# Instance-norm statistics from the loaded rows: VectorE sums and four transposes in place of sixteen matmuls

## The reference

```python
def _masked_instance_norm(x, mask):
    x = x * m                                   # m: [1, 512], over positions
    n_valid = jnp.sum(m, axis=-1)
    mean = jnp.sum(x, axis=-1) / n_valid        # one per channel
    var = jnp.sum(x * x, axis=-1) / n_valid - mean * mean
    return (x - mean) / jnp.sqrt(relu(var) + 1e-5) * m

q, k, v = Wq x + bq, Wk ctx + bk, Wv ctx + bv
attn = softmax(q k / 4, masked)
mean = attn v
std  = sqrt(relu(attn (v * v) - mean * mean))
out  = (_masked_instance_norm(x) * std + mean) * mask
```

## Time and profile before

| | us |
|---|---|
| median of 3 runs | 4275.7 (4275.27 to 4277.73) |
| the profiled execution, its own time | 4275.91 |
| its span in the trace | 4274.3 |
| first layer, from the span's start to the first instruction of the second | 703.7 |
| one batch in the steady part, g2 n = 1 to the same place of the next batch | 80.56 |

### The profile page before, as it was taken

The page is one execution under the profiler, slowest core; times in us unless marked ns, Lnnn a source line. Parts: engine busy times, 40 slices in busy tenths (PEclk is TensorE's granted clock), DMA queues, the critical chain, the costliest instruction groups (busy, mean ns, idle before and its releaser), DMA issues. The chain is left out here.

```text
span 4274.3 us, 68335 instructions
## 1 busy us (share of the span) xinstructions
PE 3998.9 (94%) x20812; PEld 3013.6 (71%) x20812; DVE 2939.8 (69%) x6467; ACT 1935.0 (45%) x3782; POOL 1592.7 (37%) x1094
## 2 busy tenths in 40 slices
PE   6999996789999987999999999999999999999999
PEld 2333333557777755887987887977988877878866
DVE  5667663688888893775757766757757757757643
ACT  3555553223333322555552555543555534545522
POOL 1334332456666651232235332344332244332330
PEclk8999998999999998999999999999999999999999
DMA  5434433000000002222223222223221123121222
GB/s 152 128 111 118 130 89 129 5 11 16 16 16 16 11 11 73 70 60 79 62 65 104 71 65 76 65 62 107 65 85 60 55 74 96 60 90 61 58 79 96
DMA packets 159993, 298.65 MB, mean 70 GB/s; under 512 B 19780, under 2 KB 42820, under 8 KB 158544
## 3 DMA queue, kind: packets, MB, share of 16 engines
q1 hardware_dynamic: 158000, 290.86, 22.1%
q0 software_dynamic: 1008, 3.67, 0.2%
q10 hardware_dynamic: 752, 1.23, 0.1%
HBM read 254.28 MB, written 42.21 MB: 69 GB/s over the span
## 5 line engine op out<-in xcount | busy, mean ns | idle before, releaser
L2176 POOL TENSOR_TENSOR c_wl<-c_wr,c_wh 128x512 fp32r<-128x512 f32 (+1 forms) x576 | 822.5, 1440 | 1640.8 <-ACT c_wh L2543 1384.6
L2644 ACT ACTIVATE c_pr<-c_ps,c_nms 128x257 f32<-128x257 f32 x512 | 244.5, 477 | 484.3 <-DVE c_nms L2866 482.4
L1700 DVE TENSOR_TENSOR_SCAN b_sb<-b_wt,b_s,b_ps 128x256 f32<-128x256 f32 x512 | 361.6, 736 | 16.0 <-PE b_ps L1153 4.1
L652 ACT ACTIVATE a_ex<-a_ps 128x1024 f32<-128x1024 f32 x256 | 260.9, 1022 | 212.8 <-PE a_ps L481 212.8
L763 DVE TENSOR_REDUCE a_nm<-a_ps 128x2 f32<-128x1024 f32 x256 | 311.5, 1221 | 60.7 <-PE a_ps L461 59.1
L1651 POOL TENSOR_TENSOR b_sb<-b_sb,b_rt 128x1024 f32<-128x1024 f32 x128 | 278.3, 2181 | 155.7 <-DVE b_sb L1700 113.3
L2543 ACT ACTIVATE c_wh<-c_wr 128x512 fp32r<-128x512 f32 (+1 forms) x464 | 315.4, 687 | 44.5 <-PE c_ps L2263 40.7
L2261 PE MATMUL c_ps<-c_hh,c_wh 128*128 128x512 f32 x768 | 309.3, 403 | 12.4 <-DVE c_hl L2750 11.9
L2261 PE MATMUL c_ps<-c_gh,c_wh 128*128 128x512 f32 x768 | 308.1, 401 | 5.4 <-DVE c_gl L2908 2.7
L2263 PE MATMUL c_ps<-c_hh,c_wl 128*128 128x512 f32 x768 | 304.3, 396 | 0.0
L2262 PE MATMUL c_ps<-c_hl,c_wh 128*128 128x512 f32 x768 | 304.0, 396 | 0.0
(11 more groups left out here) (371 smaller groups left out, 10078.7 us busy)
## 6 DMA issues: line engine op xcount, KB each, us to landing
c_wr<-in_downs SPq DMA_DIRECT2D x192, 256.0 KB, 2.7
c_wr<-in_wv SPq DMA_DIRECT2D x64, 512.0 KB, 4.0
c_wr<-in_wk SPq DMA_DIRECT2D x128, 256.0 KB, 2.9
c_wr<-in_wq SPq DMA_DIRECT2D x128, 256.0 KB, 2.7
a_qp<-strips SPq DMA_DIRECT2D x64, 256.0 KB, 4.1
a_kp<-strips SPq DMA_DIRECT2D x64, 256.0 KB, 4.9
c_wr<-in_fc SPq DMA_DIRECT2D x64, 256.0 KB, 2.8
strips<-a_qh SPq DMA_DIRECT2D x32, 256.0 KB
```

The costliest lines, as they stand in the source:

```text
L652: act.activation(EX[:, n % 4, :, :], ps[:, BT + 2 * (n % 2):BT + 2 * (n % 2) + 2, :], ACT.Exp).then_inc(ex_ready, 1)
L1700: mm = dve.tensor_tensor_scan(SB[:, quad % RING, pr % 2, e, 1:L + 1], WT[:, third(b, i), e, :], half(spread_bank(pair), e), S0[:, b % 2, 2 ...
L2176: pool.tensor_tensor(piece(WL, slot), piece(WR, slot), piece(WH, slot), ALU.subtract).then_inc(piece_cut[slot], 1)
L2644: act.activation(PR[:, i, 0:L + 1], ps[:, BS + 1 - i % 2, 0:L + 1], ACT.Exp, bias=NMS[:, i:i + 1], scale=float(K2) ** -0.5, accum_out=RS[: ...
```

## The change

The sums over positions are now made by DVE along the rows of `X`, which has channels on partitions. Each of four `tensor_tensor_reduce` writes a 128x512 product and adds it up into one column: x times the mask (`sum_inputs`, g1 n = 0 and 4, L751) and its square (`sum_squares`, g1 n = 3 and 5, L755). `column_moments` (g3 n = 4) makes mean and variance out of the columns, ACT takes the root of 128x2 numbers, DVE its reciprocal (`inverse_root`, now g0 n = 6). PE turns the columns into rows with four transposes, at the place of the sixteen matmuls, and DVE copies the bank once (`take_rows`). POOL's `normalize` subtracts and multiplies in one place in g3; `centre`, `scale`, `mask_x`, `moments`, `spread_of_x` and the squares on ACT are gone. Besides, the roots move from g0 n = 5 to n = 3, ahead of `qh`; the keys' projections from n = 4 to n = 5; `cut_x` and `cut_c` are cut in halves at two steps; `square_values` goes from n = 2 to n = 6, and that of g0 ahead of `take_pair`; SP loads the transposed x later; and the last batch's output is made by POOL for groups 0 to 2 and by DVE for group 3. Line numbers from L745 on in the diff's new functions are those of the new kernel.

```diff
-        TURN_AT, OLD_PAIR_AT, QUERIES_AT, KEYS_AT, PAIR_AT = 1, 2, 3, 4, 6
+        TURN_AT, OLD_PAIR_AT, QUERIES_AT, KEYS_AT, PAIR_AT = 1, 2, 3, 5, 6
...
                 place_maxima(b, 3)
-                load_statistics(b + 1)
                 load_inputs(b + 2)
...
                 place_maxima(b + 1, 0)
+                load_statistics(b + 1)
                 place_strips(b + 1, 3)
...
-            def centre(b):
-                pool.wait_ge(var_x, b + 1 + AHEAD)
+            def normalize(b):
+                pool.wait_ge(st_read, b + 1 + AHEAD)
                 pool.sem_inc(passed, 1)
-                pool.tensor_tensor(XM[:, :, :], XM[:, :, :], ST[:, 0:1, :].broadcast_to([P, EC, L]), ALU.subtract)
-                pool.drain().then_inc(centred, 1)
-
-            def scale(b):
-                pool.wait_ge(rstd_ready, b + 1 + AHEAD)
+                pool.wait_ge(stats_x_in, (b + 1) * N_STATS + AHEAD)
                 pool.sem_inc(passed, 1)
-                pool.tensor_tensor(XM[:, :, :], XM[:, :, :], ST[:, 3:4, :].broadcast_to([P, EC, L]), ALU.mult)
+                pool.tensor_tensor(XM[:, :, :], XT[:, :, :], ST[:, 0:1, :].broadcast_to([P, EC, L]), ALU.subtract)
+                pool.drain().then_inc(stats_read, 1)
+                pool.tensor_tensor(XM[:, :, :], XM[:, :, :], ST[:, 1:2, :].broadcast_to([P, EC, L]), ALU.mult)
                 pool.drain()
...
                     spread_out(prior)
-                    scale(prior)
...
                 group_moments(b, 2)
-                centre(b)
+                normalize(b)
                 if further:
                     cut_x(b + 2)
...
             group_3(B - 1, False, False)
+            cols = slice(0, (G0 - 1) * CG)
+            pool.wait_ge(std_ready, B + AHEAD)
+            pool.sem_inc(passed, 1)
+            pool.tensor_tensor(XM[:, :, cols], XM[:, :, cols], VAR[:, :, cols], ALU.mult)
+            pool.drain()
+            pool.tensor_tensor(XM[:, :, cols], XM[:, :, cols], MEAN[:, :, cols], ALU.add)
+            pool.drain()
+            for c in range(EC):
+                pool.tensor_scalar(OUT[:, c, cols], XM[:, c, cols], MCOL[:, c:c + 1], None, ALU.mult)
+            pool.drain().then_inc(parts_out, 1)
...
             def statistics(b):
-                pe.wait_ge(stats_in, b + 1 + AHEAD)
-                pe.wait_ge(sq_ready, b + 1 + AHEAD)
+                pe.wait_ge(cols_ready, b + 1 + AHEAD)
...
-                for c in range(EC):
-                    pe.matmul(ps[:, BX, 0:L], ONES[:, :], XM[:, c, :], start=(c == 0), stop=(c == EC - 1), skip_group_check=True)
-                for c in range(EC):
-                    mm = pe.matmul(ps[:, BX, L:2 * L], ONES[:, :], XQ[:, c, :], start=(c == 0), stop=(c == EC - 1), skip_group_check=True)
+                for i, k in itertools.product(range(2), range(LC)):
+                    mm = pe.transpose(ps[:, BX, i * L + k * P:i * L + (k + 1) * P], COLS[:, i, k:k + 1].broadcast_to([P, P]), ID[:, :])
                 mm.then_inc(st_ps, 1)
...
+                    if g == 0 and n == 0 and not first:
+                        square_values(b, 0)
                     if n == 0 and not first:
...
-                    if g == 0 and more and n == 0:
-                        cut_c(b + 1)
-                    if n == 2 and g + 1 < G0:
+                    if g == 0 and more and n in (1, 2):
+                        cut_c(b + 1, n - 1)
+                    if n == 6 and g + 1 < G0:
                         square_values(b, g + 1)
+                    if g == 0 and n == QUERIES_AT:
+                        roots(b, prior)
                     if more and g % 2 == 0 and n == QUERIES_AT:
                         queries(b + 1, g // 2)
...
-                    if g == 2 and n == 5:
-
-                        act.wait_ge(stats_in, b + 1 + AHEAD)
-                        act.wait_ge(out_free, b + AHEAD)
-                        act.activation(XQ[:, :, :], XM[:, :, :], ACT.Square).then_inc(sq_ready, 1)
-                    if g == 0 and n == 0 and not first:
-                        square_values(b, 0)
-                    if g == 0 and n == 5 and prior is not None:
-                        roots(prior)
-                    if g == G0 - 1 and n == 5 and further:
-                        cut_x(b + 2)
+                    if g == G0 - 1 and n in (5, 6) and further:
+                        cut_x(b + 2, n - 5)
...
+            def roots(b, prior):
                 act.wait_ge(var_x, b + 1 + AHEAD)
-                act.activation(ST[:, 3, :], ST[:, 2, :], ACT.Sqrt, bias=EPS[:, 0:1])
-                act.wait_ge(var_v, (b + 1) * G0 + AHEAD)
-                act.activation(VAR[:, :, :], VAR[:, :, :], ACT.Sqrt).then_inc(std_ready, 1)
+                act.activation(COLS[:, 1, :], COLS[:, 1, :], ACT.Sqrt, bias=EPS[:, 0:1]).then_inc(root_x, 1)
+                if prior is not None:
+                    act.wait_ge(var_v, (prior + 1) * G0 + AHEAD)
+                    act.activation(VAR[:, :, :], VAR[:, :, :], ACT.Sqrt).then_inc(std_ready, 1)
...
+            def sum_inputs(b, k):
+                if k == 0:
+                    dve.wait_ge(inputs_in, (b + 1) * N_IN + AHEAD)
+                dve.tensor_tensor_reduce(XS[:, k, :], X[:, k, :], M8R[:, :], 1.0, 0.0, ALU.mult, ALU.add, SUMS[:, 0, k:k + 1]).then_inc(x_summed, 1)
+
+            def sum_squares(b, k):
+                dve.wait_ge(x_summed, b * LC + k + 1 + AHEAD)
+                dve.tensor_tensor_reduce(XS[:, k, :], XS[:, k, :], XS[:, k, :], 1.0, 0.0, ALU.mult, ALU.add, SUMS[:, 1, k:k + 1]).then_inc(x_squared, 1)
+
+            def column_moments(b):
+                dve.wait_ge(x_squared, (b + 1) * LC + AHEAD)
+                dve.reciprocal(RN[:, :], NV[:, :])
+                dve.drain()
+                dve.tensor_scalar(COLS[:, :, :], SUMS[:, :, :], RN[:, 0:1], None, ALU.mult)
+                dve.drain()
+                dve.tensor_tensor(MSQ_X[:, :], COLS[:, 0, :], COLS[:, 0, :], ALU.mult)
+                dve.drain()
+                dve.tensor_tensor(MSQ_X[:, :], COLS[:, 1, :], MSQ_X[:, :], ALU.subtract)
+                dve.drain()
+                dve.tensor_scalar(MSQ_X[:, :], MSQ_X[:, :], 0.0, None, ALU.max)
+                dve.drain()
+                dve.tensor_copy(COLS[:, 1, :], MSQ_X[:, :]).then_inc(var_x, 1)
...
+                    if g == 1 and more and n in (0, 4):
+                        sum_inputs(b + 1, n // 4)
+                    if g == 1 and more and n in (3, 5):
+                        sum_squares(b + 1, n // 4)
+                    if g == 2 and more and n == 0:
+                        count_valid(b + 1)
+                    if g == 2 and n == 1:
+                        copy_mask(b)
+                    if g == G0 - 1 and more and n == 4:
+                        column_moments(b + 1)
+                    if g == 0 and n == 6:
+                        inverse_root(b)
```

More of the change, by code:

```diff
@@ L116, in layer0 @@
         MSQ = sb("msq", [P, EC, HG, D0])
-        ST = sb("st", [P, 4, L])
+        ST = sb("st", [P, 2, L])
         NV = sb("nv", [P, 1])
         RN = sb("rn", [P, 1])
+        SUMS = sb("sums", [P, 2, LC])
+        COLS = sb("cols", [P, 2, LC])
+        MSQ_X = sb("msq_x", [P, LC])
+        XS = sb("xs", [P, 2, E])
         OUT = XQ
@@ L268, in _ @@
             place_maxima(B - 1, 0)
+            load_statistics(B - 1)
             place_strips(B - 1, 3)
@@ L617, in keys, with cut_x, cut_c @@
                 act.activation(KH[:, :], ps[:, bank, :], ACT.Identity, bias=QKB[:, 1, o:o + 1]).then_inc(kh_ready, 1)
[L619 to L629, removed]
-                act.activation(CH[:, :, :], C[:, :, :], ACT.Copy).then_inc(c_high, 1)
+            def cut_x(b, k):
+                if k == 0:
+                    act.wait_ge(inputs_in, (b + 1) * N_IN + AHEAD)
+                    act.wait_ge(q_ps, b * OCT + AHEAD)
+                mm = act.activation(XH[:, k, :], X[:, k, :], ACT.Copy)
+                if k == LC - 1:
+                    mm.then_inc(x_high, 1)
+            def cut_c(b, k):
+                if k == 0:
+                    act.wait_ge(inputs_in, (b + 1) * N_IN + AHEAD)
+                    act.wait_ge(k_ps, b * OCT + AHEAD)
+                    act.wait_ge(v_ps, b * 2 + AHEAD)
+                mm = act.activation(CH[:, k, :], C[:, k, :], ACT.Copy)
+                if k == LC - 1:
+                    mm.then_inc(c_high, 1)
             def square_values(b, g):
@@ L695, in _ @@
             square_values(0, 0)
-            cut_x(1)
+            for k in range(LC):
+                cut_x(1, k)
             group(0, 0, first=True)
@@ L734, in count_valid, with inverse_root, take_rows, copy_mask @@
                 dve.drain().then_inc(mask_read, 1)
+            def sum_inputs(b, k):
+                if k == 0:
+                    dve.wait_ge(inputs_in, (b + 1) * N_IN + AHEAD)
[16 more added lines that the diff above has]
+                dve.tensor_copy(COLS[:, 1, :], MSQ_X[:, :]).then_inc(var_x, 1)
+            def inverse_root(b):
```

(22 more changed lines are left out.)

89 lines of the change are left out of this document (20 added, 69 removed).

## The result

The changed kernel takes 4304.35 us (4301.62 to 4308.96), the kernel before beside it 4275.49. The ratio is 1.0067 (interval 1.0055 to 1.0080): slower by 29 us, where 4275.5 was forecast and 4252 to 4293 given as the range.

What follows compares the result with a forecast made beforehand. PE, busy 94% of the span, was taken as the bound. Terms summed to +0.5 a batch, +3.4 over seven periods, and -3.65 outside them, giving 4275.7 against the profiled 4275.91, or 4275.5 against the median; whole range 4252 to 4293.

Steps and rivals of the forecast that it cites:

- (a): Statistics on PE: four transposes (0.66) replace sixteen matmuls (3.66); gain 3.0 us a batch.
- (b): take_rows as one copy in place of six operations of moments and spread_of_x; their waits go, gain 0.6 a batch.
- (c): In g0 the squares come ahead of take_pair and cut_c leaves that step; the wait goes, gain 1.4 a batch.
- (d): mask_x goes and count_valid in g2 about fits a step's spare time; gain 0.67 a batch.
- (h): Halved cuts, square_values at n = 6 and the later x load fit ACT's and SP's idle time; no cost.
- (f): DVE's four sums, 0.84 each against 0.60 spare, one held by POOL; loss 1.15 a batch.
- Rival D: DVE's sums run at half rate, 1.3 more a batch, 4285 us; chance 0.11.
- (g): In g3 POOL's operations hold column_moments on DVE, stalling the maxima of n = 6; loss 3.0 a batch.
- Rival B: No holding of column_moments by POOL in g3, so its 3.0 loss is 0; 4254.5 us, chance 0.32.
- C: In g3 a third POOL operation catches the column_moments chain, +2.9 a batch, 4292 us; chance 0.17.
- (e): Roots in g0: new stall of 3.9 at n = 4's weighted sums, old 1.33 and 0.60 go; loss 2.0 a batch.
- the tail: End of the last batch: POOL's groups 0 to 2, then DVE's group 3 done at 700.6, not 699.6; +1.0.

Runs made afterwards that it cites:

- e9: e5 with each of the four sums over rows replaced by setting its column to a constant; 4232.51 us.
- e5: Changed kernel with POOL's normalize waiting for column_moments and the roots at g0 n = 5 ahead of kh; 4230.11 us, ratio 0.9894.
- e4: Changed kernel with both waits left, PE repeating scores in them (nine extra pairs in g0 n = 5, seven in g3 n = 6); 4287.36 us.
- e10: Kernel before plus one unused 128x4 copy on DVE behind count_valid in g3 n = 4; 4276.83 us, ratio 1.0001.
- e7: Kernel before plus eight unused counts of the mask on DVE in g3 n = 4 of six batches; 4310.43 us, ratio 1.0077.
- e8: e7 with PE repeating the scores of n = 6 seven times in the wait; 4302.89 us, ratio 1.0063.
- e6: Kernel before plus four unused counts of the mask on DVE in g3 n = 4 of six batches; 4289.91 us, ratio 1.0033.
- e3: Changed kernel with POOL's normalize waiting for column_moments and the roots back at g0 n = 5 behind kh; 4257.66 us, ratio 0.9951.

## Why the prediction was wrong

The steps, by the differences of the groups and of a batch:

- (a), (b), (c), (d) held. g2 fell by 3.28 (the matmuls and part of (b)); g3 without the meeting fell by 1.96, where 1.4 and 0.3 of (b) were expected (the other 0.3 lies in g2; by the table's bounds the wait of 1.40 falls into g3); g1 by 0.69 in e9 and e5, where 0.67 was. In the changed kernel g1 fell by only 0.43: in three of five batches PE waited there for the transfer of the turned maxima, up to 0.74. No term had that wait ((h) put SP's side at nothing); in e4 and e5 it is not there, and what made the transfer late stays open:

```profile
351.43 0.50 PE L489 MATMUL a_ps<-a_qp,a_kp 64*128 64x512 f32 x2 [0.74 <-DMA a_qp<-a_nmT]
```

- (f) was mis-sized: +1.15 forecast, 0 measured (e9). I had charged durations (0.69 + 0.15) against spare time that I took as 0.60. What counts is the distance from one start to the next: 0.69 for a sum and its reading, 1.14 for `take_max` (its row says 1.23, but in the kernel before the one of 290.09 is followed by the next operation at 291.23), 1.83 together against a step of 1.82. And no sum was held by POOL in the changed kernel: all last 0.68. Rival D, half rate, is out: 0.68 for 512 columns. The rule on the scalar-tensor-tensor form that the forecast took from the Trainium skill ("Vector Engine (DVE) Microarchitecture Reference", Points that are easy to get wrong) isn't borne out for this operation, as its row shows; whether the rule is meant for it, which the profile lists as CUSTOM_DVE_ANT_0, stays open.
- (g) was right in mechanism and size: 2.94 of wait against 3.0, by the order of holdings that was written down. Rival B is out; C missed by 0.05 us. The Trainium skill ("SBUF — State Buffer", SBUF: two separate sides) puts it as an exclusive lock on a port pair that is held for the whole instruction, the other engine blocking fully; the rows above and those of e10 agree, 1.68 with an end 0.03 behind POOL's.
- (e) named the wait (3.9, measured 3.88) but not its path. The maxima waited, behind `qh`, `ql` and `take_max`; the forecast had counted the table load and the exponential behind `qh` and left DVE's `ql` out. The two paths are nearly of one length (325.33 and 325.74 are their ends), so the agreement is in part luck. Its own sum was also off: the terms from 311.37 on give 315.1 with the overlaps, not 315.5 (the trace has 4.0 from the variance to the exponential's end, so 315.4). No drain shows between the load (323.43, 1.28 long) and the exponential (324.72). What (e) left out is a second wait right behind the first, 0.41 for `a_ot` in e4. At full clock g0 would be 2.8 above the kernel before (23.24 against 20.43), where 2.0 was forecast.
- Outside the seven periods, the tail came at +1.2 (PE's last transposes to DVE's last operation took 9.7 us, now 11.0; forecast +1.0). One of DVE's operations in it was held by POOL for 1.4, at no cost, since DVE then waited 5.04 for POOL's maskings:

```profile
717.76 1.86 POOL L400 TENSOR_TENSOR a_xm<-a_xm,a_var 128x768 f32<-128x768 f32 x1 [3.63 <-ACT a_var L726]
718.04 1.73 DVE L898 TENSOR_SCALAR a_var<-a_msq 128x256 f32<-128x256 f32 x1
```

  The first layer's end is 26.9 us later by the profiles (726.55 against 699.6), of which seven times 3.95 are 27.7; so all that I had summed to -3.65 was in truth about -0.8. In it lies the last batch, where PE waited 3.44 (661.99) with a slow stretch of 6.4 behind it; the kernel before had there 1.82 and 3.4.

**The step that failed is the sum**: "-3.0 - 0.6 - 1.4 - 0.67 + 2.0 + 1.15 + 3.0 = +0.5" took a wait of PE at its own length. A batch grew by 3.95 instead. Put (f) at 0 and the sum is -0.7, so 4.6 are missing. Of these 3.6 are the low clock: 1.4 in g3 (23.20 against 21.76 in its own batch at full clock) and 2.2 in g0 (25.43 against the 23.24 of e4). Another 0.8 is what g0 would have lost beyond (e) at full clock, and 0.3 the transfers in g1 (rounding makes up the rest). The clock was in no term, bound or rival of mine: behind a wait of about three microseconds PE worked at 1.2 GHz for 3 to 7 us. e7 against e8 shows the same effect in isolation, e4 shows that work in the wait buys part of it back.

Seven times 3.6 is 25 us. That 4304 less these 25 comes near the 4275.5 of the forecast is luck: (f) was 1.15 too dear for each batch, g0 and g1 were 1.1 too cheap, and the part outside the periods was about 3 too good. The forecast's own range of 4268 to 4284 was also narrower than its bounds: (e) at its +3.9 alone gives 13 more, 4289.

I had the means to see it. The profile before shows no wait of PE over 1.4 in a batch of the loop, and a clock of 1.00; the only longer one, 1.82 in the last batch, was followed by four matmuls of 1.77 together, where 1.08 is usual. The forecast introduced two waits two and three times as long as any in that profile and priced them with a clock that had been measured without them. The Trainium skill ("TensorE: Matmul & The Clock Gate", Part 1, HAM oscillation) warns of just this, idle gaps that put the clock back. The runs here agree that they do, behind waits of 1.60 to 3.88.

What PE had done before the clock fell was not always the same. No wait of up to 1.5 was followed by the low clock in the kernel before, e6 or e8; one of 1.6 was in the last batch of e3 and not in that of e5; one of 1.82 was in some cases, the one of 2.47 in all of e3's batches, that of 2.9 in five of seven of the changed kernel's (not at 304.76 and 642.74), that of 3.88 in all six. Why the same wait of 2.94 is followed by the low clock in one batch and not in another stays open.

## What to carry to other kernels

Price a new wait of TensorE at its length plus a stretch at half clock if it is longer than any that the profile at hand shows at full clock. Here such a stretch cost 1.4 to 1.6 us when it lasted 3.4 and up to 2.6 when it lasted 6.8; that added 3.6 us a batch to two waits of 6.8 together, and turned a kernel about level with the old one into a slower one. When a small VectorE operation within SBUF is placed, look at what GpSimd runs then: here copies and operations of 128x2 and 128x4 were held to the end of GpSimd's, and a chain of them once for each. Not every kind is: the eight reductions of the mask in e7 took 4.83 together right beside GpSimd's 2.38. For VectorE work in spare time compare starts with starts, not the sum of durations.

## What the runs showed beside

- A held operation is not paid where there is room: e10 held DVE for 1.5 us in six batches, and the kernel's time didn't move (4276.83 against 4276.51), since a batch grew by 0.1.
- The holding goes both ways: POOL's subtraction of 128x256 took 0.99 beside a sum of DVE in g1 (343.43), 0.73 otherwise.
- Layers two to four, whose code is the same in all kernels, took from 3561 us (e5) to 3570 us (e7) in the profiles, from DVE's first operation of the second layer to the end: 3563 in the kernel before, 3569 in the changed one, 3567 in e6. It doesn't go with the first layer's length: in e9, whose first layer is as short as e5's, they took 3567. So 2 to 6 of the 29 us don't come from the first layer, and neither do some 4 of e6's. The cause stays open; no run was made for it.
